# Last stage of a tokenizer, scan and expert kernel: each scan group directly behind its weighing, and a ring of six tiles of v

## The reference

```python
delta = softplus(x @ W_D + b_D + p_Delta)
dA = delta[..., None] * A
A_bar = exp(dA)
B_bar = (A_bar - A) / dA * delta[..., None] * Bproj[:, :, None, :]
# per token:
h = a * h + b * xl[..., None]
y = einsum('bn,bdn->bd', c, h)
```

## Time and profile before

| what | value |
|---|---|
| median of 3 runs | 9341.66 us (9338.44 to 9353.73) |
| the profiled execution | 9346.65 us |
| its span, first to last instruction | 9344.9 us |
| PE, DVE, ACT, POOL busy | 7616.6, 6306.6, 4247.4, 6400.6 us |
| share of the span | 82%, 67%, 45%, 68% |
| granted TensorE clock, mean | 0.890 of full speed |

### The profile page before, as it was taken

One profiled execution on the slowest core, in us unless ns is written; L12 is line 12 of the kernel. 1 busy time (PEld: TensorE's weight loads), 2 busy tenths in 40 slices (PEclk: granted clock), 3 DMA queues, 4 the chain that ended last, 5 costly groups with the idle time before them and its releaser, 6 DMA issues.

```text
span 9344.9 us, 86112 instructions
## 1 busy us (share of the span) xinstructions
PE 7616.6 (82%) x30892; PEld 3189.1 (34%) x30892; DVE 6306.6 (67%) x8010; ACT 4247.4 (45%) x6801; POOL 6400.6 (68%) x2483
## 2 busy tenths in 40 slices
PE   6799999777999985578788778788778788777777
PEld 3444444223444432223333323333323333323333
DVE  1355555441233344888888888888888888888885
ACT  1366666553344432444444444444444444444442
POOL 0011111116766614999999999999999999999995
PEclk9999999998999987788888888888888888888887
DMA  0011111115444413223322323322323322323321
GB/s 25 25 39 43 44 42 38 31 31 105 96 102 97 101 37 99 84 95 115 108 97 91 118 90 119 108 97 89 118 90 118 110 97 89 116 93 112 110 97 51
DMA packets 356851, 786.54 MB, mean 84 GB/s; under 512 B 70437, under 2 KB 282806, under 8 KB 348936
## 3 DMA queue, kind: packets, MB, share of 16 engines
q1 hardware_dynamic: 320376, 690.75, 24.6%
q0 software_dynamic: 21712, 51.75, 2.2%
q10 hardware_dynamic: 14336, 38.54, 1.2%
HBM read 597.36 MB, written 183.35 MB: 84 GB/s over the span
## 4 chain that ended last, share of the span: by engine, by line
PE 25%; DVE 16%; POOL 9%; issue 8%; ACT 4%; DMA 0%; SPq 0%; DVEq 0%; POOLq 0%
PE ps L1492 7%; DVE v L1793 7%; DVE v L1802 7%; PE ps L1499 5%; PE ps L1497 5%; POOL v L1460 5%; POOL v L1450 4%; PE ps L1535 2%; PE ps L1488 2%; PE ps L1595 2%; DVE dl L1784 1%; ACT ps L1691 1%; ACT gm L1716 1%; ACT dl L1668 0%; DVE gm L1870 0%
## 5 line engine op out<-in xcount | busy, mean ns | idle before, releaser
L1691 ACT ACTIVATE ps<-dr,aa 128x448 f32<-128x448 f32 x2688 | 1695.8, 635 | 2649.4 <-DVE v L1802 2631.3
L1450 POOL TENSOR_TENSOR v<-xr,bt 128x1792 f32<-128x1792 f32 x672 | 2683.0, 3993 | 203.2 <-PE ps L1535 105.5
L1460 POOL TENSOR_TENSOR v<-v,ct 128x1792 f32<-128x1792 f32 x672 | 2690.2, 4003 | 177.7 <-ACT st L1681 177.1
L1802 DVE TENSOR_TENSOR_SCAN v<-ps,st,v 128x448 f32<-128x448 f32 x2304 | 2629.1, 1141 | 0.0
L1793 DVE SCALAR_TENSOR_TENSOR v<-ps,aa,v 128x448 f32<-128x448 f32 x2688 | 1786.6, 665 | 660.5 <-POOL v L1450 357.5
L222 POOL DMA_DIRECT2D tokens<-ob x448 | 235.4, 532 | 1883.4 <-ACT ob L383 1833.3
L1595 PE MATMUL ps<-w_or_w,gm 128*112 128x384 f32 x1792 | 737.2, 562 | 453.6 <-DVE gm L1870 382.2
L1535 PE MATMUL ps<-v,dg 128*32 128x448 f32 x5376 | 719.6, 610 | 218.5 <-POOL v L1460 217.9
L1595 PEld LDWEIGHTS ps<-w_or_w,gm 128*112 128x112 f32 x1792 | 340.5, 200 | 867.9 <-DVE gm L1870 424.6
L1492 PE MATMUL ps<-h,w_or_w 128*128 128x448 f32 x1344 | 538.4, 551 | 14.1 <-DVE gm L1837 14.1
L1488 PE MATMUL ps<-sq,jm 128*128 128x448 f32 x672 | 344.7, 658 | 191.2 <-ACT ot L1725 183.3
(11 more groups left out here) (318 smaller groups left out, 11777.1 us busy)
## 6 DMA issues: line engine op xcount, KB each, us to landing
xr<-h_by_channel SPq DMA_DIRECT2D x168, 896.0 KB, 4.7
dr<-delta_by_channel SPq DMA_DIRECT2D x168, 896.0 KB, 5.6
x<-tokens SPq DMA_DIRECT2D x252, 224.0 KB, 5.2
tokens<-ob POOLq DMA_DIRECT2D x448, 112.0 KB, 2.4
w_or_w<-in_w SPq DMA_DIRECT2D x29, 1536.0 KB, 6.3
w_or_w<-centred_w SPq DMA_DIRECT2D x27, 1536.0 KB, 6.4
h_by_channel<-h SPq DMA_DIRECT2D x112, 336.0 KB, 10.8
delta_by_channel<-dl SPq DMA_DIRECT2D x112, 336.0 KB, 5.1
```

The costliest lines, as they stand in the source:

```text
L1450: tt(v[:, n % RING], xr[:, dc % 2], bt[:, q:q + 1, :].to_broadcast([128, 4, T]), ALU.mult).then_inc(s_v, 1)
L1460: tt(v[:, n % RING], v[:, n % RING], ct[:, q:q + 1, :].to_broadcast([128, 4, T]), ALU.mult).then_inc(s_cm, 1)
L1691: fn(bank((4 * n + g) % 3), dr[:, dc % 2, g, :], ACT.Exp, scale=aa[:, 4 * k + g:4 * k + g + 1]).then_inc(s_a, 1)
L1802: nc.vector.tensor_tensor_scan(v[:, n % RING, g, :], bank((4 * n + g) % 3), v[:, n % RING, g, :], 0.0 if first else st[:, 4 * k + g:4 * k ...
```

## The change

1. RING is 6 instead of 5. POOL's weigh_in of step n waits for the sums of step n - 6.
2. DVE weighs group g and then scans group g, in every step. No scan is left over at the end of a step or of the last unit.
3. To make room for the sixth tile: ms is dropped and its square is written to rs2; the means of every third unit are held in rows 64 to 72 of bcs, which grows from 48 to 128 partitions and had the same bytes in each; ai, sel32, encb and wm, used in the preparation only, become parts of gm.

```diff
-RING = 5
+RING = 6
...
-        sel32 = sb("sel32", [128, 32])
-        wm = sb("wm", [128, 6])
-        ai = sb("ai", [128, 4 * STEPS])
-        encb = sb("encb", [128, CH])
-        ms = sb("ms3", [128, T])
-        bcs = sb("bcs", [48, T])
+        bcs = sb("bcs", [128, T])
-        mu = sb("mu", [128, 3, T])
+        mu = sb("mu", [128, 2, T])
...
+        ai, sel32, encb, wm = gm[:, 0, 0:4 * STEPS], gm[:, 1, 0:32], gm[:, 2, 0:CH], gm[:, 3, 0:6]
...
+        def means(i):
+
+            return mu[few, i % 3, :] if i % 3 < 2 else bcs[few, :]
...
-                    fn(mu[few, i % 3, :], ps[few, BF, 0:T], ACT.Identity, bias=mub[few, :]).then_inc(s_mu, 1)
+                    fn(means(i), ps[few, BF, 0:T], ACT.Identity, bias=mub[few, :]).then_inc(s_mu, 1)
...
-                    fn(ms[:, :], bank(BX), ACT.Square).then_inc(s_ms, 1)
+                    fn(rs2[:, :], bank(BX), ACT.Square).then_inc(s_ms, 1)
...
             def step(i, k):
                 for g in range(4):
                     weigh(i, k, g)
-                    if g > 0:
-                        scan(i, k, g - 1)
-                    elif k > 0:
-                        scan(i, k - 1, 3)
-                    elif i > 0:
-                        scan(i - 1, STEPS - 1, 3)
+                    scan(i, k, g)
...
-                    tt(bank(BS), bank(BS), ms[:, :], ALU.subtract).then_inc(s_vr, 1)
+                    tt(bank(BS), bank(BS), rs2[:, :], ALU.subtract).then_inc(s_vr, 1)
...
-                    tt(oh8, ps[few, BX, 0:T], mu[few, i % 3, :], ALU.add).then_inc(s_oh, 1)
+                    tt(oh8, ps[few, BX, 0:T], means(i), ALU.add).then_inc(s_oh, 1)
...
                     if i < UNITS:
                         step(i, k)
-                    elif k == 0:
-                        scan(UNITS - 1, STEPS - 1, 3)
```

## The result

The changed kernel takes 9274.74 us (median of 4 runs, 9272.25 to 9280.68), the kernel before 9346.51 in the same comparison (4 runs). The ratio is 0.9924, 95% interval 0.9907 to 0.9942: 0.76% or about 72 us faster. The forecast was 9238 us with a range of 9165 to 9315. The sign and the mechanism were right; the gain was 0.7 of what was forecast.

A forecast was written before the change was run, and what follows sets the result against it. No engine was taken as the bound all the time: DVE, POOL, ACT's copy and PE bound the loop in turn. The terms summed to -4.0 us a unit, 104 us over 26 loops, giving 9238 us, range 9165 to 9315.

The forecast's parts named there:

- The loop and its parts: Last stage's repeating loop, step 12 to the next unit's step 12, walked in four parts: -4.0 us a unit.
- The price of the dependency: DVE scan waiting for the weighing right in front: 0.12 us more a pair, 0.48 us a step.
- part A: Step 12 to the states of step 19, DVE the bound: changes of -0.55, -0.55, +0.11, +0.96 and -1.52 us.
- The bound from above: Most a dependent weighing and scan pair on DVE was taken to cost extra: 0.19 us.
- Part B: From there to step 3 of the next unit, POOL running almost without waits: -0.94 us, with no margin.
- The slower rival: DVE becomes the bound; at 0.24 us more a weighing the loop is +3.0 us a unit, 9420 us; chance 0.13.
- Part C: At step 3, ACT's copy that PE idles for comes earlier: -1.52 us a unit.
- Part D: From ACT's copy to step 12, PE working without a gap through projection and experts: change 0.
- The sixth tile: All 75 POOL waits for PE vanish, but only one is on the loop: 0.94 us a unit.
- The shared buffers: Buffers laid into others: same engines and sizes, no new wait, costed at nothing.
- rival on PE's clock: PE's clock stays at 2.4 GHz behind the shortened idle time at step 3: -6.3 us a unit, 9178 us; chance 0.11.
- the dependency is free: Rival: a scan waiting for its weighing costs nothing extra; -7.6 us a unit, 9144 us; chance 0.02.

The follow-up runs named there:

- Run 4: Changed kernel with DVE's wait for the states kept one unit earlier moved ahead of each step's first weighing; 9264.94 us, ratio 0.9906 to the kernel before.
- run 5: Changed kernel with DVE order weigh 0, weigh 1, scan 0, weigh 2, scan 1, weigh 3, scan 2, scan 3; 9214.73 us.
- run 10: Changed kernel with POOL's weighing-out of step k - 3 in place of k - 2; 9253.38 us, ratio 0.9892 to the kernel before.
- run 7: Changed kernel with ACT's last copy of a unit's output at step 2 of the next unit, not step 3; 9284.5 us, ratio 0.9931 to the kernel before.
- run 2: Changed kernel with DVE's old order put back, six tiles and shared buffers kept; 9310.15 us, ratio 0.9959 to the kernel before.
- run 1: Changed kernel with five tiles in the ring in place of six; 9304.92 us, ratio 0.9949 to the kernel before.
- run 6: The kernel of run 5 with five tiles in the ring in place of six; 9214.29 us, ratio 0.9853 to the kernel before.
- run 3: Kernel before with only the shared buffers: old order, five tiles; 9346.27 us, ratio 0.9995 to the kernel before.
- run 8: The kernel of run 5 with POOL's weighing-out of step k - 3 in place of k - 2; 9111.29 us, ratio 0.9745 to the kernel before.

## Why the prediction was right, and where its size was off

*The loop and its parts* held. All seven stretches came out with the forecast sign or zero, and the forecast changes of waits came too: rs1 3.13 to 1.11 us (1.2 forecast), step 18 gone.

*The price of the dependency* was the term that was mis-sized. The prediction had 0.12 us a pair from L1775 and L1777, and 0.48 us a step. The plain pair measured 0.12 (0.70 against 0.58), and the scan itself lasts 1.150 us where it had 1.141. But the first scan of each step waits for two semaphores and starts 0.78 us behind its weighing, where 0.60 lay before: 0.18. A step is 0.58 us dearer (two steps, 19.38 - 18.22 = 1.16). Run 4 shows the 0.07 us of it that are the second wait. In part A this makes -0.76 us out of the forecast -1.55: the missing 0.8 us a loop are nearly the whole miss of 0.9 a loop. The bound from above, 0.19 a pair, held: the mean over a step is 0.14. The "like kind of pair" was of an instruction with one wait, and the mis-sized step was to take its price for all four.

*Part B without margin*: -0.83 for -0.94. DVE comes to step 3 without waiting for POOL, which the prediction named as a sign of being wrong. It is the forecast at its edge: runs 5 and 10 show that POOL's pace and DVE's dearer one give nearly the same there, 47.65 and 47.80 us. The 0.94 was reckoned from POOL's wait, and what ends the stretch in the changed kernel is DVE's pace; that this came to nearly the same size is in part luck. The slower rival began here, but its price of 0.24 a pair was not reached.

*Part C* held (-1.46 for -1.52), and run 7 shows that ACT's copy is what ends PE's wait. *Part D* held at zero; the tight place was real: PE waits 0.34 us once in it for DVE's first gm.

*The sixth tile*: 0.97 us a loop alone (run 2, forecast 0.94), 1.0 in the mean with the order of the change (run 1, 48.82 against 47.78 us to step 3), nothing with the better order (run 6). The prediction took POOL's 0.94 us wait for PE as it stood; behind it were products below full clock, at a place that its rival on PE's clock did not name. *The shared buffers*: nothing (run 3).

*From the loop to the time*: 26 loops of 3.14 would be 82 us. The loop into a new image gains less (198.30 to 196.10), and the last stage as a whole is 78 us shorter: from POOL's first instruction to the end of its last, 5606.3 against 5528.0 us. The stages ahead, whose code is the same, took 7 us longer in this profiled run (POOL's first instruction at 3644.7 against 3637.5); over all the kernels run here this start lies between 3628.7 and 3649.4, so it belongs to no edit.

*The other rivals.* That the dependency is free is refuted by run 5, which gets 0.58 us a step back by order alone. The Trainium skill, page "VectorE: DVE Perf Modes", section "The DRAIN you can't avoid", says of a chain of eight tensor_copy that the semaphores between them cost nothing extra. Here, between ops of 448 float32, a wait for the op in front costs 0.12 us and a second wait in front of the same op 0.07. The same section also says that a next op that is not held starts earlier, so the overlap of 0.08 us does not speak against it, as the prediction had it. PE's clock at the squares did not stay up: 4.66 us at a granted clock of 0.53, for 4.85 at 0.50, after 6.19 us idle; over the 25 loops it is 3.9 to 4.9 us.

## What to carry to other kernels

Ask two things apart when an order is changed: what the new neighbourhood costs, and what the new end of the block gives. Here a scan that ends in its own step frees banks and states for two other engines, and an order was to be had that gives this without putting any instruction directly behind the one it waits for. Where two engines take turns as the bound, more distance between them pays only as far as each one's own pace leaves room: the same lag took 4.3 us off the stretch to step 3 where DVE's own pace was short enough (run 8), and nothing where DVE alone needs 47.8 us for it (run 10). In time it was worth 1.1% with one order and 0.3% with the other.

## What the runs showed of the hardware

- Two DVE instructions of 448 elements overlap by 0.08 us when nothing ties them; a wait for the one in front costs 0.12 us from start to start, a second wait, long fulfilled, 0.07 more. In front of a weighing, which waits for nothing that DVE did just before, that same wait cost nothing.
- After idle time of 0.96 to 2.4 us PE's next piece ran now at a granted clock of 0.61 to 0.67 (up to 4.53 us) and now at full clock (2.83 us). The length of the idle time alone did not tell which.
- Where the squares were moved out from behind a gap (run 7), they ran at full clock (2.49 us), and the products now behind the gap ran below it: 6.31 us at 0.75 in place of 4.78. Work taken out from behind a gap can leave the bill to the next.
